# Block attention and norm at the end of a four-part kernel: the projection added by TensorE as one row per batch element, tiles in eight PSUM banks, no copies of x with projection or beta

## What is computed

```
block_repr = inputs.reshape(B, n_blocks, block_size, H).sum(axis=2)      # 8 x 8 x 512
keys = jnp.einsum('bnh,kh->bnk', block_repr, Wk)
rms = jnp.sqrt(jnp.mean(keys * keys, axis=-1, keepdims=True) + EPS)
scores = jnp.einsum('bnh,h->bn', keys / rms * rms_weight, q)
attn = softmax(scores)                                                   # over the 8 blocks
attended = jnp.einsum('bn,bnh->bh', attn, block_repr)                    # one row per batch element
proj = jnp.einsum('bsh,kh->bsk', broadcast(attended), Wo)
x = inputs + proj
out = (x - mean(x)) / sqrt(var(x) + EPS) * ln_gamma + ln_beta
result = inputs + out
```

## Time and profile before

| | |
|---|---|
| median of three runs | 1946.95 us (1944.41 to 1948.63) |
| the profiled execution | 1949.1 us, its span 1947.1 us |
| TensorE clock granted, mean of the span | 0.962 |
| busy: PE, DVE, ACT, POOL | 95%, 65%, 56%, 19% |
| end of the recurrence (last POOL instruction) | 1891.45 us |
| first and last instruction of VectorE on a tile | 1914.82 and 1943.49 us |

### The profile page before, as it was taken

One profiled execution on the slowest core, in us unless ns is written; L12 is line 12 of the kernel. 1 busy time (PEld: TensorE's weight loads), 2 busy tenths in 40 slices (PEclk: granted clock), 3 DMA queues, 4 the chain that ended last, 5 costly groups with the idle time before them and its releaser, 6 DMA issues. The chain is left out here.

```text
span 1947.1 us, 87066 instructions
## 1 busy us (share of the span) xinstructions
PE 1852.5 (95%) x33006; PEld 1410.3 (72%) x33006; DVE 1262.5 (65%) x5545; ACT 1092.0 (56%) x4107; POOL 379.4 (19%) x1398
## 2 busy tenths in 40 slices
PE   7977999999999999999989999999999999999996
PEld 2434464565646556464658999999999999999995
DVE  7445474746747474673254777777777777777767
ACT  0342737557473654748544666666565656566545
POOL 3000000000000000000002334343434343433335
PEclk7688999999999999999988999999999999999997
DMA  6121314232131323212331000000000000000002
GB/s 210 57 83 42 96 32 102 68 85 85 32 107 32 100 71 77 77 25 63 109 109 30 1 1 0 0 0 0 0 0 0 0 0 0 0 0 1 0 0 87
DMA packets 103590, 86.73 MB, mean 45 GB/s; under 512 B 15681, under 2 KB 90561, under 8 KB 103505
## 3 DMA queue, kind: packets, MB, share of 16 engines
q1 hardware_dynamic: 102480, 85.43, 15.4%
q0 software_dynamic: 384, 0.01, 0.0%
q10 hardware_dynamic: 640, 0.13, 0.0%
HBM read 60.20 MB, written 21.00 MB: 42 GB/s over the span
## 5 line engine op out<-in xcount | busy, mean ns | idle before, releaser
L1326 PE MATMUL bank_pair_A<-moving,rep 128*128 128x16 f16 x8192 | 317.7, 169 | 2.4 <-ACT bank_pair_C L1417 1.4
L1326 PE MATMUL bank_pair_B<-moving,rep 128*128 128x16 f16 x8192 | 315.5, 169 | 0.0
L1326 PE MATMUL bank_pair_C<-moving,rep 128*128 128x16 f16 x8192 | 315.5, 169 | 0.0
L1326 PEld LDWEIGHTS bank_pair_A<-moving,rep 128*128 128x128 f16 x8192 | 276.5, 96 | 12.7 <-issue 4.0
L1426 ACT ACTIVATE r_gate<-r_pre 128x16 f32<-128x16 f32 x512 | 110.5, 216 | 288.9 <-DVE r_pre L1506 288.9
L1326 PEld LDWEIGHTS bank_pair_B<-moving,rep 128*128 128x128 f16 x8192 | 259.0, 96 | 0.0
L1326 PEld LDWEIGHTS bank_pair_C<-moving,rep 128*128 128x128 f16 x8192 | 259.0, 96 | 0.0
L1313 PE MATMUL bank_pair_D<-x_part,w_in 128*128 128x256 f16 x1536 | 197.0, 273 | 2.6 <-DVE x_part L1478 2.6
L1506 DVE TENSOR_REDUCE r_pre<-bank_pair_A 128x16 f32<-128x32 f32 x512 | 98.2, 192 | 138.4 <-PE bank_pair_A L1326 138.4
L1212 POOL TENSOR_TENSOR x<-x,w_in 128x512 f32<-128x512 f32 x8 | 10.2, 1272 | 878.6 <-DMA w_in<-w_in 878.6
L1099 DVE TENSOR_REDUCE head_max<-bank_pair_A 128x2 f32<-128x1024 f32 x128 | 155.9, 1218 | 34.2 <-PE bank_pair_A L611 34.0
(11 more groups left out here) (264 smaller groups left out, 3777.2 us busy)
## 6 DMA issues: line engine op xcount, KB each, us to landing
rep<-parts SPq DMA_DIRECT2D x256, 64.0 KB
parts<-parts SPq DMA_DIRECT2D x44, 256.0 KB, 2.1
q_rep<-parts SPq DMA_DIRECT2D x32, 256.0 KB, 4.8
k_rep<-parts SPq DMA_DIRECT2D x64, 128.0 KB, 2.8
parts<-parts SPq DMA_DIRECT2D x40, 128.0 KB, 2.6
w_in<-in_x_dram SPq DMA_DIRECT2D x8, 512.0 KB, 3.8
x<-in_x_dram SPq DMA_DIRECT2D x8, 512.0 KB, 4.1
w_in<-w_in SPq DMA_DIRECT2D x128, 32.0 KB, 2.0
```

Source lines behind the costliest of these rows:

```text
L1326: last = nc.tensor.matmul(ps[part][:, o:o + 2 * B], w[:, k, (first + c) * P:(first + c) * P + P], moving[j % 2][:, k, :, :].rearrange("p s ...
```

## The change

`xp` and `xb` are gone, and so is `ln_shift`. A tile is brought from `xT` into one PSUM bank by four f32 products with `ident` (products now, so that more can be added on top; `transpose` is no longer used for them). An f16 tile `added` holds per partition row either a projection (rows 0 to 7 rounded, rows 32 to 39 the rest), beta (row 64 rounded, row 96 the rest) or zero. An f16 product with a selector `sel_proj` as stationary operand and `added` as moving operand, 512 columns, adds one batch element's projection to a whole tile (`add_rows(.., y_ps)`). After ScalarE has written mean - x to SBUF (`apart`), a second such product with `sel_back` takes the projection off again and adds beta in the same bank (`back_ps`). GpSimd multiplies `apart` by -gamma into `scaled`, and VectorE ends with one instruction: scaled x rstd + bank. The 16 tiles go round eight banks; VectorE runs `result` four tiles behind `statistics`, with `moments` behind `result`.

The softmax's weights are transposed by TensorE, and the projection is a product with them (`dens`, `projected`), divided on the way out of PSUM. The projection of the sums is now four products with 512 moving columns. The selectors are made by two GpSimd instructions of 128x1024, and VectorE has some ten more small instructions at its start. At the end of the recurrence TensorE runs eight more 128x256 products and then already brings the first two tiles. Beta is loaded as two rows on the SyncE queue at the start of the recurrence.

```diff
@@ recurrence, sync
-            for tile, row in zip(columns, (cond[1:2, :].rearrange("a n -> (a n)"), rms_w, beta)):
+            for tile, row in zip(columns, (cond[1:2, :].rearrange("a n -> (a n)"), rms_w)):
...
+            for row in (BETA_HI, BETA_LO):
+                sp.dma_start(beta_rows[row:row + 1, :], beta.rearrange("(a n) -> a n", a=1)).then_inc(norm_ld, 16)
@@ recurrence, tensor
             blocks(pe, step, product)
+            for n in range(8):
+                nc.tensor.matmul(pG[1], w_in[0][:, n % DC, 0:P], w_in[1][:, n % DC, 0:B * TB], start=True, stop=True)
+            for b in range(2):
+                for c in range(DC):
+                    nc.tensor.matmul(pD[:, b, c * P:c * P + P], xT[:, c, b, 0:P], ident[:, :], start=(c == 0), ...
@@ block_attention, tensor
+            def project_sums(c):
+                return nc.tensor.matmul(rows, sumsT[c], woT[:, c, :], start=(c == 0), stop=(c == DC - 1), skip_group_check=True)
...
+            def transposed(i):
+                b, tc = TILES[i]
+                if i >= len(BANKS):
+                    pe.wait_ge(res_ok, i - len(BANKS) + 1)
                 for c in range(DC):
+                    nc.tensor.matmul(BANKS[i % len(BANKS)][:, c * P:c * P + P], xT[:, c, b, tc * P:tc * P + P], ident[:, :], ...
+            def add_rows(i, selector, done):
+                nc.tensor.matmul(BANKS[i % len(BANKS)], selector[:, TILES[i][0], :], added[:, :], start=False, stop=True,
+                                 skip_group_check=True).then_inc(done, 1)
...
+            for i in range(T):
+                pe.wait_ge(apart_ok, i + 1)
+                add_rows(i, sel_back, back_ps)
+                if i + AHEAD < T:
+                    if i + AHEAD >= len(BANKS):
+                        transposed(i + AHEAD)
+                    add_rows(i + AHEAD, sel_proj, y_ps)
@@ block_attention, scalar
+            for i in range(T):
+                act.wait_ge(mv_ok, i + 1)
...
+                nc.scalar.activation(apart[i % len(apart)][:, :], BANKS[i % len(BANKS)], ACT.Identity, bias=mv[:, i, 0:1], scale=-1.0).then_inc(apart_ok, 1)
+                if i % 2 == 1:
+                    rstd(i - 1)
@@ block_attention, vector
+            nc.vector.tensor_copy(own[:, PROJ_LO:M], own[:, 0:B]).then_inc(qw_ok, 1)
+            nc.vector.tensor_copy(own[:, B:PROJ_LO], own[:, 0:1].broadcast_to([R, PROJ_LO - B])).then_inc(qw_ok, 1)
+            nc.vector.tensor_scalar(gamma_neg[:, :], gamma_bc[:, :], -1.0, None, ALU.mult).then_inc(qw_ok, 1)
...
+                nc.vector.scalar_tensor_tensor(out=res[:, i, :], in0=scaled[i % len(scaled)][:, :], scalar=ln_rstd[:, i:i + 1],
+                                               in1=BANKS[i % len(BANKS)], op0=ALU.mult, op1=ALU.add).then_inc(res_ok, 1)
...
+            for i in range(T + LAG):
+                if i < T:
+                    statistics(i)
+                if i >= LAG:
+                    result(i - LAG)
+                if i < T:
+                    moments(i)
@@ block_attention, gpsimd
+            pool.wait_ge(qw_ok, 4)
+            nc.gpsimd.tensor_copy(sel_proj[:, :, :], plus[:, :].unsqueeze(2).broadcast_to([P, B, P])).then_inc(sel_ok, 1)
+            nc.gpsimd.tensor_tensor(sel_back[:, :, :], of_beta[:, 0:1].unsqueeze(2).broadcast_to([P, B, P]), ...
+            pool.wait_ge(qw_ok, 7)
+            for i in range(T):
+                pool.wait_ge(apart_ok, i + 1)
...
+                nc.gpsimd.tensor_tensor(scaled[i % len(scaled)][:, :], apart[i % len(apart)][:, :], gamma_neg[:, :], ALU.mult).then_inc(g_ok, 1)
```

More of the change, by code:

```diff
@@ L1662, in block_attention @@
[L1662 to L1669, removed]
@@ L1670, in block_attention @@
[L1670 to L1677 removed]
+        own = t("own", [R, M])
+        weights = t("weights", [R, M])
@@ new lines, in block_attention @@
+        block_proj = t("block_proj", [R, D])
+        inverse = t("inverse", [M, 1])
+        added = t("added", [P, D], F16)
+        plus = t("plus", [P, B])
+        of_beta = t("of_beta", [P, 1])
+        sel_proj = t("sel_proj", [P, B, P], F16)
+        sel_back = t("sel_back", [P, B, P], F16)
+        gamma_neg = t("gamma_neg", [P, D])
+        stats = t("stats", [P, B * NC, 6])
+        mv = t("mv", [P, B * NC, 2])
+        ln_rstd = t("ln_rstd", [P, B * NC])
+        apart = [t(f"apart{n}", [P, D]) for n in range(4)]
@@ L1679, in _ @@
+        block = ctx.enter_context(nc.Block())
+        TILES = [(b, tc) for tc in range(NC) for b in range(B)]
+        BANKS = [pD[:, 0, :], pD[:, 1, :], pB[:, 0, :], pB[:, 1, :], pC[:, 0, :], pC[:, 1, :], pA[:, 0, :], pA[:, 1, :]]
+        AHEAD = 6
+        LAG = 4
+        keys, sums, turned, dens = pA[:, 0, 0:DC * R], pA[:, 0, DC * R:DC * R + 2 * R], pB[0:R, 0, 0:P], pB[0:M, 1, 0:1]
+        rows = pA[0:R, 1, :]
+        projected = pC[0:M, 0, :]
+        T = len(TILES)
         @block.sync
@@ L1720, in tile_of @@
-            def tile_of(src, bank, b, tc):
-                for c in range(DC):
-                    last = nc.tensor.transpose(bank[:, tc, c * P:c * P + P], src[:, c, b, tc * P:tc * P + P], ident[:, :])
-                return last
-            def projected(b):
-                for elements, done in XP:
-                    if b in elements:
-                        pe.wait_ge(done, (b + 1 - elements[0]) * DC)
-            pe.wait_ge(xb_act, XB_ACT)
-            pe.wait_ge(xb_dve, DC - XB_ACT)
@@ new lines, in _ @@
+            project_sums(0)
+            pe.wait_ge(sq_ok, 1)
+            pe.wait_ge(dot_ok, 1)
+            pe.wait_ge(consts, 3)
+            for c in range(DC):
+                last = nc.tensor.matmul(sums, ones[:, :], key_sq[:, c, :, :].rearrange("p s r -> p (s r)"), start=False, stop=(c == DC - 1),
+                                        skip_group_check=True)
+            last.then_inc(sum_ps, 1)
+            for c in range(1, DC):
+                last = project_sums(c)
+            last.then_inc(rows_ps, 1)
@@ new lines, in _ @@
+            dve.wait_ge(qw_ok, 6)
+            dve.wait_ge(wt_ps, 1)
+            nc.vector.tensor_tensor(weights[:, :], turned[:, 0:M], own[:, :], ALU.mult).then_inc(wt_ok, 1)
+            dve.wait_ge(pj_ps, 1)
+            nc.vector.reciprocal(inverse[:, :], dens).then_inc(inv_ok, 1)
+            dve.wait_ge(hi_ok, 1)
+            nc.vector.scalar_tensor_tensor(out=added[PROJ_LO:M, :], in0=projected[PROJ_LO:M, :], scalar=inverse[PROJ_LO:M, 0:1],
+                                           in1=added[PROJ_LO:M, :], op0=ALU.mult, op1=ALU.subtract).then_inc(lo_ok, 1)
```

268 lines of the change are left out of this document (106 added, 162 removed).

## The result

The changed kernel took 1930.8 us (median of 4 runs, 1929.16 to 1934.38) beside 1945.68 us of the kernel before on the same chip (4 runs, 1944.04 to 1948.63). The ratio is 0.9924, 95% interval 0.9908 to 0.9941: 14.9 us less, where 9.6 were forecast.

A forecast was written before the change was run, and what follows sets the result against it. TensorE at half clock bounds the front, VectorE the tiles. Front 23.0 to 18.1 (-4.9), barrier +0.5, tiles 32.3 to 27.05 (-5.2): 9.6 us off the 1946.95 median gives 1937.4 us; range 1931.5 to 1941.5.

The forecast's parts named there:

- The barrier's cost: End of the recurrence: products added ahead of the barrier make TensorE start the next stage 0.5 us later.
- S: Start of TensorE's first product behind the barrier, forecast at 1892.35 us; later front times are counted from it.
- The keys at full clock: Front: the keys' 32 records run at clock 1.00 instead of 0.50, done 3.6 us after TensorE's start.
- that rival: Tiles: the result waits for GpSimd because its row scalar counts as second SBUF input; 1943.3 us, chance 0.09.
- The slower rival: Tiles: TensorE stays at half clock, 2.65 us a tile; about 1954.2 us, chance 0.04.
- VectorE's start: Front: VectorE's small instructions wait for GpSimd's two large ones, putting `dot_ok` at S + 7.6, bounds 4.5 and 9.
- idles 3.4 us, so the sums at half clock: Front: TensorE's wait before the sums drops its clock to 0.50; eight records take 1.8 us, ending at S + 9.5.
- the no-wait rival: Front: VectorE gets ahead of GpSimd and the clock holds; first statistics at S + 13.05, 1932.3 us, chance 0.20.
- the tail and the end: Tiles: work behind the last moments, 3.1 us, then stores and the span's end, 2.9 us.
- TensorE is just so: Tiles: TensorE needs 1.3 us a tile, only just below VectorE's 1.43 us.
- removed copies: Front: `xp` stood on the path to the first statistics, `xb` beside other work; counted within the old 23.0 us.
- The slower rival's threshold: Tiles: with the half-clock front, TensorE's time decides from a tile above 1.8 us on.

The follow-up runs named there:

- the run with 3.62 us: Changed kernel with VectorE's casts of beta behind three large GpSimd instructions (`sel_back` made twice), so TensorE idles longer before the sums; stage 45.17 us, trace only.
- The run with the kernel before: Kernel before plus 18 f16 products that nobody reads, between the recurrence's last step and the barrier; ratio 0.9952 to the kernel before.
- 2.22 us a tile: Changed kernel with the four f32 products that bring a tile issued twice, from the third tile on; stage 51.61 us, trace only.
- the run with the late selectors: Changed kernel, but GpSimd makes its two selectors only after VectorE has written both halves of beta; ratio 0.9925 to the kernel before.

## Why the prediction was too small

**Right.** The barrier's cost: S came 0.52 us later against R, forecast 0.5. The keys at full clock, forecast 3.6 us, 3.76 measured. VectorE waits behind GpSimd at the start of the stage. `ln_shift` as the place where VectorE waited in the tiles, and that the new result, with a row scalar from SBUF, does not: 709 to 748 ns, most of the sixteen beside a busy GpSimd and the last (1929.40) with GpSimd done at 1929.27, so that rival falls. The slower rival falls too: the clock is 1.00 as long as TensorE brings tiles.

**The front was forecast at S + 18.1 and came at S + 14.73: 3.4 us of the miss.** The step that failed is "VectorE's start", `dot_ok` at S + 7.6. It came at 1898.28 + 0.43 = 1898.71, S + 5.8. Two things were wrong in it. GpSimd's instructions were over at S + 4.3, not at S + 5.3: they began 0.55 earlier and took 3.5 us, not 3.9. And behind them stood 1.0 us of work, not 1.9: the two copies and `gamma_neg` ran unhindered beside GpSimd's first instruction, and the casts were held up during GpSimd's time, so that only 0.28 us of the second and the subtraction (0.69) came after it. The forecast had every instruction of VectorE wait from the first on. The rule that issue order decides who blocks, which the prediction cited from the Trainium skill (page "SBUF — State Buffer", section "Who interferes with whom"), was applied to one side only.

The step behind it then failed by itself: "idles 3.4 us, so the sums at half clock". TensorE stood idle for 1.13 us and kept 1.00; the run with 3.62 us shows what the forecast described, at the forecast size. From the start of the sums the changed kernel needed 8.8 us to the first statistics, against 10.4 with half clock and 8.45 in the no-wait rival. So 1.8 us of the miss come from the later `dot_ok` and 1.6 from the clock.

**The tiles were forecast at 27.05 and took 25.05: 2.0 us.** The mechanism was right and the terms were too dear: rounds of 1.33, not 1.43 (12 rounds, 1.2 us), since memset and aggregate cost 0.09 between their neighbours and not 0.22, while the result cost 0.66 and not 0.61; the first four 3.36, not 3.8; the tail and the end 5.7, not 6.0 (1932.70 less 1907.65 + 3.36 + 15.96). That "TensorE is just so" at 1.3 us a tile proved harmless.

**What was right by luck.** The front's gain was explained as several parts of one rearrangement. The run with the kernel before shows that 7.3 of its 7.74 us need only the eighteen idle products. The prediction did count the keys at full clock; but "removed copies" as a cause of the front's gain is small: 0.4 us net. With the 0.5 lost at the barrier and the 1.16 in the casts given back, the front is 13.97, which is 2.1 us less than the old front at full clock.

**The slower rival's threshold** ("decides from a tile above 1.8 us on") was tried at one value only. With 2.22 us a tile TensorE does set the round once the banks are used up, and still the stage is 4.0 us shorter than before. That run has a front of 18.31 us, though, and not the rival's, whose first statistics come 25.3 us behind S. With S at R + 0.90 and the same tiles it would be 0.90 + 25.3 + 33.30 = 59.5 us (an estimate), longer than the 55.65 before. So the run doesn't show the threshold to be wrong.

**The range.** The no-wait rival gave 1932.3 and a chance of 0.20; the time lies 1.5 us below it, but not by its mechanism. It was a mixture that I had not listed: a wait, but one too short for the clock to fall. The rival itself is what the run with the late selectors shows: no wait, and the first statistics at S + 13.58, where it had S + 13.05. The range allowed for tiles dearer than forecast and not for cheaper ones; 2.0 us less there would have taken its lower end to 1929.5.

One sum is off by little: the terms of the tiles, 3.8 + 17.2 + 3.1 + 2.9, make 27.0 and not 27.05.

The Trainium skill, page "SBUF — State Buffer", section "Who interferes with whom", says that a `tensor_reduce` of VectorE never contends with GpSimd, while an instruction with two inputs in SBUF does beside a GpSimd instruction that reads SBUF. The traces agree: 154 ns against a median of 930 in the same place.

## What to carry to other kernels

Look at the granted clock on both sides of every barrier: if TensorE goes in idle and comes out at 0.50, try to give it work up to the barrier (real work if there is some, or products that nobody reads), short enough to end before the engine that the barrier waits for. Where VectorE has a short instruction with two SBUF inputs inside a loop beside GpSimd, its length is GpSimd's, not its own; recast it so that one input comes from PSUM or as a row scalar, or drop it. When two engines may lock each other, write out who begins first for each instruction, on both sides, before summing waits.

## What the runs showed of the hardware that I had not expected

- The clock is held much more easily than it is regained. F32 products of 64 columns kept 1.00 when they began at it (32 records in 3.76 us), and stayed at 0.50 when they began at it (7.06 us, and in all 11.9 us of work of several shapes before the clock rose).
- When the clock falls after TensorE goes idle varies. After 1.64 us of idle time ahead of the sums it was still 1.00. After 3.62 us it was 1.00 for another 0.5 us of work and only then 0.50. Ahead of the barrier in the kernel before, the last work ended at 1889.4 and 1890.5 already shows 0.50. That is within 1.1 us of the last work. What makes the difference was not settled.
- The lock between VectorE and GpSimd works both ways within one microsecond: `sel_proj` 1.44 instead of 1.04 us for GpSimd, and casts of 1.14 and 2.00 instead of 0.42 for VectorE. `gamma_neg` took 0.41 us beside GpSimd's cast and 0.41 with GpSimd idle, so the delay fell on GpSimd.
- A cast of a single row of 512 elements takes 0.42 us, as long as 128 rows of the same width do in `gamma_neg`.
